# Moving the normalised expert-layer rows of the causal units from VectorE to ScalarE in a two-layer attention and expert kernel

## The reference

```python
x = layernorm(x + local_attention(x, w_qkv, w_out))      # 16 heads of 8, keys at most 128 tokens back
# block with causal attention and a layer of 8 experts
h = layer_norm(x, ln1_g, ln1_b)
x_resid = x + causal_attention(h) @ w_o
moe_in = layer_norm(x_resid, ln2_g, ln2_b)
probs = softmax(moe_in @ w_gate); two best experts per token, weights made to sum to 1
out = sum of gate_e * (gelu(moe_in @ w1[e] + b1[e]) @ w2[e] + b2[e])
x = layernorm(x + out + x_resid)
```

## Time and profile before

| | us |
|---|---|
| median of 3 runs | 760.44 (759.86 to 764.75) |
| the profiled execution, its own time | 760.87 |
| span of the profiled execution, first to last instruction | 759.1 |
| busy in the span: TensorE, VectorE, ScalarE, GpSimd | 627.7, 565.8, 463.0, 420.9 |

### The profile page before, as it was taken

One profiled execution on the slowest core, in us unless ns is written; L12 is line 12 of the kernel. 1 busy time (PEld: TensorE's weight loads), 2 busy tenths in 40 slices (PEclk: granted clock), 3 DMA queues, 4 the chain that ended last, 5 costly groups with the idle time before them and its releaser, 6 DMA issues.

```text
span 759.1 us, 20439 instructions
## 1 busy us (share of the span) xinstructions
PE 627.7 (83%) x7679; PEld 386.6 (51%) x7679; DVE 565.8 (75%) x1265; ACT 463.0 (61%) x774; POOL 420.9 (55%) x646
## 2 busy tenths in 40 slices
PE   3568998999988788998889888889677996999960
PEld 1333544544544443444444434444226996999950
DVE  2565786888878889898989888988633775566656
ACT  3046775777766476767676767666763573456534
POOL 5026666667765454244647464757755545555753
PEclk9569998999999999999999999999978998899985
DMA  6744843754652627263536363621221223222645
GB/s 199 188 122 98 196 140 60 196 143 105 137 149 53 165 77 149 85 118 106 138 104 140 106 139 89 155 63 26 62 60 43 68 61 88 72 68 75 138 94 166
DMA packets 59004, 84.31 MB, mean 111 GB/s; under 512 B 7848, under 2 KB 48272, under 8 KB 55836
## 3 DMA queue, kind: packets, MB, share of 16 engines
q1 hardware_dynamic: 52284, 68.78, 35.9%
q0 software_dynamic: 6336, 13.71, 7.6%
q10 hardware_dynamic: 288, 0.52, 0.2%
HBM read 43.55 MB, written 37.17 MB: 106 GB/s over the span
## 4 chain that ended last, share of the span: by engine, by line
PE 49%; DVE 16%; issue 9%; DMA 8%; ACT 8%; POOL 4%; SPq 3%; another core or an unknown queue 1%; POOLq 0%; ACTq 0%; DVEq 0%
PE side_ps L1502 10%; PE pair_ps L1651 8%; PE pair_ps L1663 8%; ACT probs L762 5%; PE pair_ps L1425 5%; DMA arena<-parts_dram 5%; DVE row_max L938 4%; PE pair_ps L1523 4%; DVE row_max L940 2%; PE pair_ps L1482 2%; PE side_ps L1562 2%; DMA arena<-shift_t 2%; PE pair_ps L1476 2%; SPq L489 2%; POOL rows_dram L672 2%
## 5 line engine op out<-in xcount | busy, mean ns | idle before, releaser
L762 ACT ACTIVATE probs<-pair_ps 128x1024 f32<-128x1024 f32 x272 | 275.9, 1022 | 125.5 <-PE pair_ps L1425 117.5
L1502 PE MATMUL side_ps<-probs,v_aug 128*32 128x256 f32 (+3 forms) x2048 | 161.0, 410 | 9.1 <-POOL probs L660 4.1
L889 ACT ACTIVATE arena<-pair_ps,arena 128x128 f32<-128x128 f32 x284 | 81.0, 369 | 77.8 <-PE pair_ps L1651 45.8
L647 POOL TENSOR_SCALAR_AFFINE_SELECT probs<-probs 128x512 f32<-128x512 f32 x96 | 61.4, 640 | 112.2 <-ACT probs L762 111.3
L1425 PE MATMUL pair_ps<-arena 50*128 50x256 bf16 (+3 forms) x1024 | 107.2, 285 | 19.5 <-DMA arena<-shift_t 7.1
L929 DVE TENSOR_REDUCE row_max<-pair_ps 128x4 f32<-128x768 f32 x96 | 89.1, 950 | 27.2 <-PE pair_ps L1459 26.7
L713 POOL DMA_INDIRECT outputs_dram<-arena x71 | 70.9, 999 | 66.8 <-DVE arena L1293 35.2
L1651 PE MATMUL pair_ps<-arena 128*128 128x128 f32 x568 | 80.3, 287 | 11.5 <-DVE arena L1282 7.2
L1425 PEld LDWEIGHTS pair_ps<-arena 50*128 50x128 bf16 x1024 | 32.3, 95 | 99.5 <-issue 46.7
L938 DVE TENSOR_REDUCE row_max<-pair_ps 128x2 f32<-128x1024 f32 x64 | 76.7, 1219 | 8.3 <-PE pair_ps L1482 5.9
L1663 PE MATMUL pair_ps<-pack,arena 128*128 x568 | 78.2, 283 | 3.8 <-ACT arena L889 3.2
(11 more groups left out here) (178 smaller groups left out, 1007.6 us busy)
## 6 DMA issues: line engine op xcount, KB each, us to landing
arena<-parts_dram SPq DMA_DIRECT2D x96, 192.0 KB
parts_dram<-parts SPq DMA_DIRECT2D x32, 384.0 KB
parts_dram<-parts SPq DMA_DIRECT2D x32, 256.0 KB
pack<-in_pack SPq DMA_DIRECT2D x8, 578.0 KB, 10.0
arena<-rows_dram SPq DMA_DIRECT2D x71, 65.0 KB
parts_dram<-parts SPq DMA_DIRECT2D x32, 128.0 KB
arena<-parts_dram SPq DMA_DIRECT2D x32, 128.0 KB
resid<-outputs_dram POOLq DMA_DIRECT2D x6, 512.0 KB
```

Of the source, the lines that this page charges most:

```text
L762: nc.scalar.activation(probs[:, n % PROBS, :], pair_ps[RING_AT["score", n][0]][:, :, :].rearrange("p b t -> p (b t)"), ACT.Exp, scale=SCAL ...
L889: last = nc.scalar.activation(hidden[n % H_DEPTH][:, f * BLK:(f + 1) * BLK], hidden_ps[n % 2][:, f * BLK:(f + 1) * BLK], ACT.Gelu_apprx_ta ...
L1502: last = nc.tensor.matmul(o_ps[c * VHEAD:(c + 1) * VHEAD, q0:q0 + width], v_aug[u % 2][:, j, first:first + VHEAD], probs[:, slot, r * T + ...
```

## The change

For units 8 to 14 VectorE no longer makes the rows. At step 11 (`NEGATE`), after R(11), it makes only `neg_mean` = -mean * rstd, 128 x 4 values, as soon as `rstd` is there. ScalarE makes the rows at step 12, behind X(12) and `copy_o` and ahead of X(13), as `Identity(scale * y + bias)` with scale = rstd and bias = neg_mean: four instructions of 128 x 128 f32. The waits for the buffer `rows` move with them from VectorE to ScalarE. Unit 15 is left as it was.

```diff
+NEGATE = 11
 APPLY = {LOCAL: 5, CAUSAL: 12}
...
+        neg_mean = sb("neg_mean", [P, NT])
...
+            def apply_rows(w):
+
+                b = w - B
+                act.wait_ge(negated, b + 1)
+                if b:
+                    act.wait_ge(misc_filled, JOB["xf", w - 1])
+                    act.wait_ge(rows_out, b * (CHOICES * 16))
+                    act.wait_ge(rows_copied, b)
+                for t in range(NT):
+                    last = nc.scalar.activation(rows[:, 0, t, 0:C], y[:, t, :], ACT.Identity, scale=rstd[:, 0, t:t + 1],
+                                                bias=neg_mean[:, t:t + 1])
+                last.then_inc(applied, 1)
...
                     if project_at(it, k - 1) is not None:
                         middle_part(project_at(it, k - 1))
+                    if real(w) and layer(w) == CAUSAL and k == APPLY[CAUSAL]:
+                        apply_rows(w)
                     if real(w) and layer(w) == CAUSAL and k == 16:
                         copy_rows(w)
...
+            def negate(w):
+
+                dve.wait_ge(rstd_done, w + 1)
+                if w > B:
+                    dve.wait_ge(applied, w - B)
+                nc.vector.scalar_tensor_tensor(out=neg_mean[:, :], in0=mean_var[:, :, 0], scalar=-1.0, in1=rstd[:, 0, :],
+                                               op0=ALU.mult, op1=ALU.mult).then_inc(negated, 1)
...
-                    if real(w) and layer(w) == CAUSAL and k == APPLY[CAUSAL]:
-                        apply(w)
+                    if real(w) and layer(w) == CAUSAL and k == NEGATE:
+                        negate(w)
```

More of the change, by code:

```diff
@@ L403, in build @@
         rstd_done, h_part_done, x1_ready = sem("rstd_done"), sem("h_part_done"), sem("x1_ready")
+        negated = sem("negated")
         applied, sum_ready = sem("applied"), sem("sum_ready")
```

## The result

The changed kernel takes 772.66 us (median of 4 runs, 767.37 to 773.13), the kernel before beside it 762.6 (4 runs, 759.86 to 765.53). The ratio is 1.0119, with an interval of 1.0079 to 1.0159: slower by some 9 us (10.1 between the medians; the recorded ratios are not the quotients of the medians, from which they differ by up to 0.3% here). Forecast was 767.3, with a range of 763.5 to 770.3, and the measured median lies outside it. The profiled execution took 772.31 us of its own time (span 770.5), 11.4 more than the one of before.

The account below looks back on a forecast made before the run. No engine was full; the wait chain lay on TensorE, with 0.46 us of slack at X(13). Losses of 4.52 (four times 1.13), 1.34, 1.00 and 0 made 6.9 us on 760.87, 767.7, less 0.4: 767.3, range 763.5 to 770.3.

Parts of the forecast that it names:

- Step 1: Step 12 of an iteration: four row instructions leaving VectorE (1.11 us) give back 0, since TensorE itself is busy.
- Step 2: VectorE between R(11) and R(12): `neg_mean` takes 0.16 us without a stall, hidden by the products with V, cost 0.
- Step 3: ScalarE ahead of X(13): the four row instructions take 1.65 us and move X(13) by 1.54 us.
- Step 4: TensorE at M(14): X(13), with 0.46 us of slack, makes M(14) and all behind it 1.13 us late per iteration.
- Step 5: ScalarE's list in iterations 10 and 12: the moved wait for scattered DMAs makes the losses 1.34 and 1.00 us.
- Step 6: Iteration 15: the delay of X(13) is hidden by 1.75 us of idle time before X(14), loss 0.
- A: Rival: VectorE is the bound, so freeing it gains 0.95 us six times, 5.7 us, giving 754.7; chance 0.06.
- B: Rival: slack later in the iteration takes the loss back, half or none staying, 760.4 to 764; chance 0.14.
- C: Rival: larger loss, from late DMAs in iterations 11, 13, 14 (769.5) or TensorE's lower clock (769 to 771); chance 0.20.

Follow-up runs that it names:

- Insertion alone: Kernel before plus four ScalarE instructions ahead of X(13) writing to a tile nobody reads, VectorE keeping its rows: 745.07 us, ratio 1.009.
- relief alone: Kernel before with three of VectorE's four row instructions left out and ScalarE untouched: 738.41 us, ratio 1.0007.
- the kernels with two buffers: Changed kernel and kernel before, each with `rows` as two tiles used in turn: 768.31 us, ratio 1.0092, and 761.05 us, ratio 0.9979.
- the dose: Kernel before with two `rows` buffers plus 3 to 8 unread ScalarE instructions ahead of X(13) in iterations 9 to 14: 771.39 us, one run.
- the repeat: Changed kernel and kernel before, both unchanged, run once more: 750.26 us, ratio 1.0156, and 737.81 us, ratio 1.0008.
- the kernel before again: Kernel before, unchanged, run once more: 737.81 us, ratio 1.0008.

## Why the prediction was right or wrong

**Step 1, right.** Four row instructions off VectorE give back 0. Insertion alone loses as much in a clean iteration as the changed kernel does, and relief alone gains only where VectorE waits for the DMAs.

**Step 2, right.** `neg_mean` took 0.15 us, nothing waited for it.

**Step 3, right.** 1.65 us for the four was the price of the earlier trace rows, and 1.65 us is measured. X(13) starts 1.55 us behind their start (forecast 1.54).

**Step 4, right in place and size.** M(14) waits for X(13) in every clean iteration (0.96 us), and the loss is 1.12 at step 14, of which 0.09 comes back in the same iteration. The forecast of 1.13 leaves this 0.09 out. The six times 1.05 between the kernels with two buffers and the line of the dose show both parts of the term, the 0.38 each and the slack.

**Step 5 failed, in what it put behind the wait.** It ended with S(15): it did not ask what TensorE does while X(13) is held up by 1.54 and the DMA wait together. TensorE stands idle for 1.89 us there (2.04 and 2.06 on the chip of the repeat), and the clock behind that falls to its lower level. The sum has this term at nothing. It measured about 1.5 us in iteration 10 of the first profile, and 3.4 and 1.5 in iterations 10 and 12 of the repeat. Two buffers take away the wait and the clock together.

The delay up to S(15), which is what the step did cost, was 1.8 and 0.47 us where it says 1.34 and 1.00: each is off by half a microsecond, and the sum is right by luck. On the chip of the repeat it was 1.13 and 1.07. The landing was sized from one profile: "landing is no later than 374.99" and "the last of these DMAs lands 7.89 us after its issue". The chain of waits of the changed kernel has these two pieces, iterations 10 and 12:

```profile
368.08 7.82 DMA rows_dram<-rows,row_at
...
448.36 7.31 DMA rows_dram<-rows,row_at
```

In iteration 10 it was later than the 7.5 us that the forecast took, in iteration 12 earlier than the 7.89. The 0.09 for taking up the wait has no row behind it; from these landings to the rows (376.06 and 455.83) it is 0.16.

So the stretch of the first profile adds up like this: clean iterations 4.2 (forecast 4.52), delay of iterations 10 and 12 up to S(15) 2.3 (2.34), clock 1.5 (0), in all 7.99 (6.86). In the repeat it is 4.1, 2.2 and 4.9, in all 11.2.

**Step 6, right.** Iteration 15 loses nothing at step 14 (-0.02).

**The rivals.** A is dead: the kernel that only relieves VectorE is at 1.0007, and the insertion costs the same with the relief and without. VectorE is the fullest engine of the earlier trace rows by busy share, 33.98 of 38 us, and taking work off it is worth 0 all the same. The Trainium skill, page "Perfetto Trace Analysis", section "Optimizing Scalar/DVE Operations", says that moving work from a saturated VectorE to ScalarE may make sense; the runs here do not bear it out. B is seen only as the 0.09. C is half of what happened. Its mechanism, the lower clock after a wait of TensorE, came, but not for the reason it gives, an idle time of 1.1 us before each M(14): after the waits of 0.95 us in the clean iterations the clock never fell. Its other half, late DMAs in iterations 11, 13 and 14, did not come at all. It was given 0.20, and it was held against it that the clock is 1.00 in the earlier trace rows. But the earlier trace rows is of a kernel in which TensorE has no wait of more than 1 us in that iteration; it says nothing on what the clock does once there is one. The place to look was the two iterations in which the DMA wait and the four instructions stand one behind the other.

**The rest.** Step 5 does not explain the whole miss. The first two profiles are 11.4 us apart where 6.9 was forecast; 1.1 of the missing 4.5 us lie in the stretch, and 3.4 outside it, where their cause is not shown. And the time of before moved from 760.44 to 762.6 with the fourth run, which no step of a sum can foresee: on the time that the forecast started from, the ratio of 1.0119 gives 769.5. On the chip of the repeat the loss of 11.5 us is 4.6 above the forecast, and the clock there is worth 4.9. The forecast ratio was 767.3 / 760.44 = 1.009, and insertion alone has the same 1.009. That is no confirmation: insertion alone loses only 4.1 us in the stretch, nothing in iterations 10 and 12, and the rest of its ratio lies elsewhere.

## What to carry to other kernels

Before work goes to the engine that has time to spare, look at the place in its list: the room is the start of the first thing that waits for it less the end of what it waits for (0.46 us here, confirmed by one to eight instructions), and not the idle time of the whole iteration (10 us here). Look also at which waits move along. A wait for a DMA that cost 1.3 to 2.0 us of the stretch in VectorE's list holds up everything behind it in ScalarE's, and adds to the work there instead of running beside it. A second buffer takes the wait away (3.0 and 6.9 us of the stretch here).

## What the runs showed of the hardware that was not expected

- TensorE's granted clock fell from 2.4 to 1.2 GHz after single waits of 1.72, 1.89, 2.04 and 2.06 us in iterations that otherwise kept it. It did not fall after 2.10 and 2.49 us, nor after 1.38 us and less. After the 1.72 it stayed low from 459 to 467 us at least. What decides is open; no run here set out to vary anything but the length of the wait.
- In iterations 10 and 12 the last of the eight scattered DMAs lands between 7.2 and 8.2 us after its issue (7.19 with one row moved, 8.20 in the kernel before again). In iterations 11, 13 and 14 of the changed kernel the rows start 7.05 us after the issue without a wait, so it had landed sooner, in both profiles. Why these two iterations are late is open.
- On one of the chips all four profiles take 157 to 160 us from the last `o_norm_t` to the end, and on the others it is 174 to 179; the granted clock of the kernel before is 1.00 from 620 to 680 us there and 0.91 in the first profile. Iteration 15 is shorter too. Whole times can only be compared with the kernel before on the same chip.
